# Graph layer on one core: a gather ring of eight thirds instead of six, key/value work six thirds later, weights loaded where they are used

## What is computed

```python
xn = _layernorm(x, axis=-1)
x = x + _L0_gnn_ref(xn, edge_attr_256, src, dst, gnn_weights, gnn_h_bias, 6250) \
      + _L0_mix_ref(xn[None], w_qkv, ..., w1, b1, w2, b2)[0]
x = x + _L0_ffn_ref(_layernorm(x, axis=-1)[None], Wr, br, W1, b1, W2, b2, gamma, beta)[0]
...
# gnn: over 106,250 edges sorted by dst
m = src_feats[src_idx] @ weights[:d] + edge_feats @ weights[d:]
norm = where(deg > 0, rsqrt(max(deg, 1)), 0)
h = segment_sum(m * norm[dst_idx][:, None], dst_idx) + h_bias
# mix: linear attention with 8 heads, layer norm of k and v
kv = einsum('bhnd,bhne->bhde', ln(k), ln(v)) / HW
h = gelu((einsum('bhnd,bhde->bhne', q, kv) + x) @ w1 + b1) @ w2 + b2 + x
# ffn: one router for all rows picks 2 of 8 experts (256 -> 512 -> 256)
```

## Time and profile before

| | |
|---|---|
| three runs | 1624.92, 1627.36 (median), 1629.15 us |
| the profiled execution | 1632.06 us |
| its span | 1630.3 us |
| granted TensorE clock, mean share | 0.872 |
| busy in the span | PE 1173.3, PEld 803.1, POOL 915.7, DVE 654.6, ACT 559.7 us |
| moved | 295.03 MB, mean 181 GB/s |

### The profile page before, as it was taken

How to read it: one execution, slowest core, us unless ns; L and a number is a source line. 1 busy time by engine, 2 the same in 40 slices (tenths; PEclk the granted TensorE clock), 3 DMA queues, 4 the chain that set the end, 5 groups by cost and what they waited for, 6 DMA issues and landing times.

```text
span 1630.3 us, 22836 instructions
## 1 busy us (share of the span) xinstructions
PE 1173.3 (72%) x7416; PEld 803.1 (49%) x7416; DVE 654.6 (40%) x1698; ACT 559.7 (34%) x1157; POOL 915.7 (56%) x975
## 2 busy tenths in 40 slices
PE   0157767776686777766676767677776839999997
PEld 0033333433343343334445444453554539999997
DVE  5633223323223333221233244243432446676775
ACT  4731111111111111111333343333342457677674
POOL 6166666666666666666666666666666103344342
PEclk9988987888788888778798897889898959999999
DMA  9976666656665666486677787777777341222221
GB/s 234 319 216 202 181 194 185 205 177 180 201 193 174 189 199 181 127 260 204 206 225 232 220 240 248 225 223 241 234 225 238 103 136 40 71 61 76 64 68 39
DMA packets 209235, 295.03 MB, mean 181 GB/s; under 512 B 20940, under 2 KB 180146, under 8 KB 207887
## 3 DMA queue, kind: packets, MB, share of 16 engines
q1 hardware_dynamic: 152899, 165.66, 34.7%
q0 software_dynamic: 39888, 108.97, 22.1%
q10 hardware_dynamic: 16350, 19.20, 3.5%
HBM read 261.75 MB, written 32.00 MB: 180 GB/s over the span
## 4 chain that ended last, share of the span: by engine, by line
another core or an unknown queue 31%; PE 30%; issue 14%; DVE 9%; ACT 9%; DVEq 2%; DMA 2%; SPq 2%; ACTq 1%; POOL 0%; POOLq 0%
PE bank L1156 8%; PE bank L1167 8%; PE bank L944 2%; PE bank L997 2%; PE bank L938 2%; DVEq L1324 2%; PE bank L930 2%; PE bank L1003 1%; ACT fl L649 1%; PE bank L1041 1%; ACT L751 1%; ACT L731 1%; DVE acc L1326 1%; DVE xc L1339 1%
## 5 line engine op out<-in xcount | busy, mean ns | idle before, releaser
L583 POOL DMA_INDIRECT ring<-xn_table,src_sb x807 | 781.8, 969 | 465.7 <-issue 221.1
L930 PE MATMUL bank<-ring,s 128*32 128x512 f32 x1662 | 283.6, 667 | 65.3 <-DVE s L1298 42.6
L944 PE MATMUL bank<-fl_t,wg 128*128 128x128 f32 x1120 | 158.7, 300 | 51.6 <-ACT fl_t L649 36.7
L944 PEld LDWEIGHTS bank<-fl_t,wg 128*128 128x128 f32 x1120 | 146.7, 211 | 54.8 <-ACT fl_t L649 38.8
L938 PE MATMUL bank<-ident,fl 128*128 128x128 f32 x280 | 60.9, 356 | 146.9 <-ACT fl L649 131.7
L1326 DVE TENSOR_TENSOR acc<-acc,bank 128x96 f32 x277 | 70.7, 255 | 226.5 <-issue 87.4
L938 PEld LDWEIGHTS bank<-ident,fl 128*128 128x128 f32 x280 | 39.3, 177 | 222.2 <-ACT fl L649 170.7
L1331 DVE TENSOR_TENSOR xt_lo<-bank,xt_hi 128x250 fp32r<-128x250 f32 (+1 forms) x75 | 37.9, 505 | 260.7 <-ACT xt_hi L649 173.0
L649 ACT ACTIVATE xt_hi<-bank 128x250 fp32r<-128x250 f32 (+1 forms) x75 | 33.4, 446 | 285.6 <-remote 227.3
L712 ACT ACTIVATE kvn<-xc 125x512 f32<-125x512 f32 x50 | 31.5, 630 | 262.1 <-DVE xc L1339 135.3
L1156 PE MATMUL bank<-xf_hi,fw_hi 128*128 128x256 f32 x400 | 113.5, 284 | 9.4 <-DVE fw_lo L1628 7.2
(11 more groups left out here) (221 smaller groups left out, 2374.1 us busy)
## 6 DMA issues: line engine op xcount, KB each, us to landing
ring<-edges SPq DMA_DIRECT2D x207, 512.0 KB
ring<-xn_table,src_sb POOLq DMA_INDIRECT x807
xnr<-xn_table SPq DMA_DIRECT2D x50, 125.0 KB
xnr<-xn_table SPq DMA_DIRECT2D x25, 250.0 KB
xch<-x SPq DMA_DIRECT2D x25, 250.0 KB
base_rows<-xch ACTq DMA_DIRECT2D x25, 250.0 KB
x_rows<-xch ACTq DMA_DIRECT2D x25, 250.0 KB
xt_cols<-xte ACTq DMA_DIRECT2D x25, 250.0 KB
```

The costliest lines, as they stand in the source:

```text
L583: pool.indirect_dma_start(out=to, out_offset=None, in_=rows, in_offset=bass.IndirectOffsetOnAxis(ap=index, axis=0),).then_inc(done, 16)
L930: mm = pe.matmul(ps_seg[t % 2][j * W:(j + 1) * W, :], lhsT=s32[:, t % 3, j * TS + i, :].bitcast(F32), rhs=ring[:, u, j, :], start=i == 0, ...
L944: mm = pe.matmul(ps_y[:, o * P:(o + 1) * P], lhsT=wg[:, c, o * P:(o + 1) * P], rhs=fl_t[:, c, :], start=c == 0, stop=c == 3)
```

## The change

The ring gets two more slots, and 32 KB per partition are found for them by laying buffers over each other. `RAW`, which was `RS`, stays at six. KV0 goes from 2 to 8; through it FOLD becomes 112, MIX runs from 120 to 207, and FIN from 42 to 71 (the number of steps stays 225). SP issues the weights at the steps at which they are next needed, and DVE and ACT prepare the kv weights at step 7, inside the loop.

```diff
-RS = 6
+RS = 8
...
-RAW = RS
+RAW = 6
...
-KV0 = 2
+KV0 = 8
...
-        xch = sbe("xch", [TN, XC, 2, D])
...
+        chunk_rows = sbm("chunk_rows", [P, XC, 2, D])
...
+        xch = chunk_rows[0:TN, :, :, :]
+        fold_flat = chunk_rows[:, :, :, :].rearrange("p c j d -> p (c j d)")
+        wq_sb, w1_sb, p_sb = (fold_flat[:, k * KC * D:(k + 1) * KC * D].rearrange("p (c d) -> p c d", d=D) for k in range(3))
...
@@ SP, mix_load @@
                 if c < XN:
                     sp.wait_ge(s_xt, NT)
+                    sp.wait_ge(s_c, 6)
...
@@ SP @@
             for q in range(RAW):
+                if q == 3:
+                    sp.wait_ge(s_rel, 1)
+                    sp.dma_start(wg[:, :, :], wgnn.rearrange("(c p) d -> p c d", p=P)).then_inc(s_wg, 16)
                 edge_load(q)
-            sp.wait_ge(s_rel, 1)
...
             sp.wait_ge(s_tab, TABLE_DONE)
...
             for q in range(TS * STEPS):
                 if RAW <= q < NQ:
                     edge_load(q)
+                if q == RAW:
+                    key_weights()
+                if q == RAW + 2:
+                    mix_weights()
...
@@ ACT @@
             for h in range(2):
...
-                act.wait_ge(s_gve, h + 1)
-                nc.scalar.activation(sdg[:, tiles], veg[:, tiles], ACT.Sqrt).then_inc(s_gsd, 1)
-                act.wait_ge(s_gr, h + 1)
+                act.wait_ge(s_vx0, NB + h + 1)
+                nc.scalar.activation(sdg[:, tiles], veg[:, tiles], ACT.Sqrt).then_inc(s_sx0, 1)
+            for h in range(2):
+                tiles = slice(h * RAW * ST // 2, (h + 1) * RAW * ST // 2)
+                act.wait_ge(s_r1, NB + h + 1)
...
-            act.wait_ge(s_wprep, 2)
-            copy(wkv_hi[:, :, :], wstage[:, :, :]).then_inc(s_wsplit, 1)
...
+                if q == KV0 - 1:
+                    act.wait_ge(s_wprep, 2)
+                    copy(wkv_hi[:, :, :], wstage[:, :, :]).then_inc(s_wsplit, 1)
...
@@ PE @@
                     if t == 1:
-                        pe.wait_ge(s_par, 16 * 11)
+                        pe.wait_ge(s_wg, 16)
...
@@ DVE @@
-            raw_stats(0)
-            raw_stats(1)
-            raw_scales(0)
-            raw_scales(1)
...
+            one_hot(0)
+            raw_stats(0)
+            raw_stats(1)
+            raw_scales(0)
+            raw_scales(1)
...
+                    if t == 1:
+                        v.wait_ge(s_zero, 1 + NB)
                     sums(t - 1)
+                if q == KV0 - 1:
+                    key_weights()
+                if q == KV0 + 6:
+                    row_bias()
```

More of the change, by code:

```diff
@@ L234, in gps_layer @@
         DEG = 3 * P
+        xch = chunk_rows[0:TN, :, :, :]
+        fold_flat = chunk_rows[:, :, :, :].rearrange("p c j d -> p (c j d)")
+        wq_sb, w1_sb, p_sb = (fold_flat[:, k * KC * D:(k + 1) * KC * D].rearrange("p (c d) -> p c d", d=D) for k in range(3))
+        kv_t = fold_flat[:, 3 * KC * D:3 * KC * D + KC * P].rearrange("p (c n) -> p c n", n=P)
+        floor = fl[0:1, 0:NS]
+        st6 = fl[0:TN, 288:288 + 6 * BLK].rearrange("p (j s) -> p j s", s=6)
+        mvs = fl[0:TN, 352:352 + 4 * BLK].rearrange("p (h j s) -> p h j s", h=2, s=2)
+        RT = RAW * ST
+        raw_flat = fl_t[:, :, :].rearrange("p c n -> p (c n)")
+        st6g = raw_flat[:, 0:6 * RT].rearrange("p (k s) -> p k s", s=6)
+        mvg = raw_flat[:, 6 * RT:8 * RT].rearrange("p (k s) -> p k s", s=2)
+        veg, sdg, rg, nmrg = (raw_flat[:, k * RT:(k + 1) * RT] for k in range(8, 12))
         sum_row = kvn[0:1, :, :].rearrange("p a (b d) -> p (a b) d", d=D)
@@ L258, in gps_layer @@
             "st", "mv", "vx0", "sx0", "rc0", "r1", "xn", "xnp", "tab", "zero"))
-        s_gst, s_gmv, s_gve, s_gsd, s_grc, s_gr, s_raw = (sem(f"s_{n}") for n in ("gst", "gmv", "gve", "gsd", "grc", "gr", "raw"))
-        s_id, s_const, s_iota, s_mask, s_d, s_dp, s_rel, s_wprep, s_wsplit = (sem(f"s_{n}") for n in (
-            "id", "const", "iota", "mask", "d", "dp", "rel", "wprep", "wsplit"))
+        s_raw = sem("s_raw")
+        s_id, s_const, s_iota, s_mask, s_d, s_dp, s_rel, s_wprep, s_wsplit, s_wg = (sem(f"s_{n}") for n in (
+            "id", "const", "iota", "mask", "d", "dp", "rel", "wprep", "wsplit", "wg"))
         s_e, s_gat = ([sem(f"s_{n}{u}") for u in range(RS)] for n in ("e", "gat"))
@@ L464, in _, with key_weights @@
-            sp.dma_start(hrows[:, :], hbias.partition_broadcast(TN)).then_inc(s_par, 16)
-            sp.dma_start(wr_sb[:, :, :], wr.rearrange("(c p) e -> p c e", p=P)).then_inc(s_rw, 16)
-            sp.dma_start(rt[0:1, 0, :], br.partition_broadcast(1)).then_inc(s_rw, 16)
-            sp.wait_ge(s_tab, TABLE_DONE)
+            sp.wait_ge(s_tab, TABLE_DONE)
+            def key_weights():
+                sp.dma_start(wstage[:, :, :], wkv_l.rearrange("(c p) d -> p c d", p=P)).then_inc(s_wkv, 16)
+                sp.dma_start(bkv[:, :], bkv_l.partition_broadcast(TN)).then_inc(s_wkv, 16)
+                for j, row in enumerate((kln_g, vln_g, kln_b, vln_b)):
+                    sp.dma_start(lns[:, j, :], row.partition_broadcast(P)).then_inc(s_par, 16)
@@ L958, in fold_weights @@
                 if step == 0:
+                    pe.wait_ge(s_par, 16 * 10)
                     pe.wait_ge(s_cs, 4)
```

86 lines of the change are left out of this document (38 added, 48 removed).

## The result

| | before | after |
|---|---|---|
| median of the runs | 1626.14 us (4 runs) | 1635.13 us (4 runs, 1634.52 to 1638.71) |
| ratio, 95% interval | | 1.0052 [1.0032, 1.0072] |
| profiled execution, span | 1632.06, 1630.3 us | 1638.71, 1636.9 us |
| third 8 summed | 117.2 us | 112.7 us |
| third 206 summed | 1289.5 us | 1284.3 us |

What follows compares the result with a forecast made beforehand. It took the bound to be a cycle: PE's completions arrive late while POOL streams gathers, with the ring full of landed data. Terms −14 +5 +0 −3 +2 +2 = −8 gave 1619.4 us on the median; 8-in-10 range 1600 to 1635.

Steps and rivals of the forecast that it cites:

- mix six steps later: Last thirds and tail: MIX ends at 207, not 201, so two more chunks fall there; +2 us, bounds 0 and +5.
- the start: Before the loop and its first steps: without early kv work third 8 is summed at about 103.6; −14 us, bounds −17 and −8.5.
- filling the slots: Early loop: POOL issues 8 more gathers before first pausing, while PE's completions are late; +5 us, bounds 0 and +10.
- the prediction's own sign of being wrong: Early loop: third 8 summed later than 110 us, where near 104 would show the forecast right.
- fold gate: SP at step 120: `mix_load(0)` waits for step 118, edge loads queue behind, at most one delay; +2 us, bounds 0 and +6.
- third rival: Early loop: filling the ring takes 10 us and eats the start's gain; −3 us in all, 1624.4, no change; chance 0.14.
- Steady state: Main loop: two more landed thirds give PE nothing, period stays 5.9 to 6.0 us per third; 0, bounds −5 and +5.
- The reading behind it: Main loop: PE's completions reach others late while POOL streams gathers; the cycle's cost per third does not contain the ring's depth.
- The first rival: Main loop: pauses are a lack of slots, period falls from 5.95 towards 5.1; total 1450, or 1565 for a third; chance 0.12.
- The rival that made the kernel slower through the gate: SP at step 120: first edge load lands after 12 us, PE stands; price 12 to 15, 1631.4 to 1634.4; chance 0.12.
- End of the gathers: Last thirds, run without gathers at 4.6 us instead of 5.95: two more such thirds; −3 us, bounds −4 and 0.

Runs made afterwards that it cites:

- lead of six: Changed kernel with POOL's gathers held to six thirds ahead of PE, SP's edge loads keeping eight slots: 1632.13 us, ratio 1.0029 against the kernel before.
- second set: Changed kernel run again beside the kernel before on a 5.9 us chip, unaltered: 1633.72 us against 1627.34, ratio 1.0033.
- paced kernels: Changed kernel with mix chunks 9/8 of a group apart instead of 6/5; with eight slots 1480.63 to 1484.84 us on 5.07 us chips, ratios 1.0046 to 1.0067.

## Why the prediction was wrong

**The failed step is "mix six steps later, +2, bounds 0 and +5".** The tail grew by 11.7 us, and by 13.1 in the second trace. I had put PE's work of a chunk at some 4 us and taken the tail for a place where a little of it lies bare. Two terms were too small. First, two more chunks in the last thirds can lay twice that work bare, 8 us, by the prediction's own figure, and the bound was +5; from third 206 to the last projection 7.9 us more were measured. Second, the closings were not in the sum at all: four chunks are turned behind the last projection, not two, one after the other, about 4 us each, and that gives 4.1 us more. What stands between two turns is a chain through PE, DVE and ACT. The table of group numbers in the source would have told the count ahead: with FIN starting at 42 the last four closings are at 68 to 71, so that four turns fall behind the last edges.

That the placing of the side work makes the loss is shown: KV0 = 2 takes it away (1.0003 against 1.0033 and 1.0052 on 5.9 us chips, 0.9987 and 0.9992 against 1.0061 on 5.07 us chips), and KV0 = 8 alone puts it on the kernel before (1.0103), with the tail of the changed one.

**The second step that failed is the start, −14, with +5 for filling the slots.** Third 8 came at 112.7 and 110.1, so −4.5 and −7.1 of the −14, and the prediction's own sign of being wrong, third 8 later than 110, came true. That it came at 103.0 with a lead of six does not make the size right for six slots: there the same late signal only falls behind third 9, and by third 12 all three stand 6 to 7 us ahead of before. So the mechanism behind the +5 was right (PE's signals are late while POOL streams), but it is not the two more slots that bring it on. By third 206 the loop was to be 12 us ahead (−14, +5 and −3, not counting the fold gate); by the medians it is about 3 us ahead (estimated above), and by the same reckoning 7 us in the second set. Third 8 was also no fair milestone: by then the kernel before has done kv work that the changed one does later. My third rival (−3 in all, no change) described the loop up to there better than the forecast.

**Steady state, 0: right.** 5.92 against 5.91 us per third, 90 pauses. The reading behind it (completions are seen late while gathers stream) held against its rivals: the half-gather run, the signal at 108.27, and the updates of one kernel on two chips say the same. The first rival, pauses for lack of slots, falls on this chip. The Trainium skill, Perfetto Trace Analysis, section on optimization strategy, has the repeated gap as a possible sign of too few buffers; here the gaps stayed at eight slots (123.8 and 73.3 us), so here it was not that.

**Fold gate, +2 with bounds 0 and +6: held.** SP was held for 26 us (35 forecast), and PE waited once, 4.95 us at third 121, without falling behind; in two more traces there was no such wait. The rival that made the kernel slower through the gate did not occur. The sign of the result came from a place for which I had no rival.

**End of the gathers, −3:** not separable from the start in the traces; the changed kernel sums thirds 201 to 206 at 4.1 us each (1263.7 to 1284.3), the one before at 4.6.

## What to carry to other kernels

Where side work rides on a loop by fixed steps, moving its first step moves its last one, and what falls behind the loop's end has no cover: count the dependent closings behind the last shared step, engine by engine, before pricing the start. A buffer ring that is full of landed data gains nothing from depth, and a head start that nobody on the critical path waits for is not passed on. One early milestone can mislead about such a head start; look at a few later ones too. Packing the side work closer to save the tail can give the saving back inside the loop.

## What the runs showed of the hardware

The kernel before took 1474 to 1476 us on some chips and 1625 to 1627 on others (medians), with gathers of the same length. On the slower ones PE's semaphore updates came late while POOL issued gathers back to back: those behind the projections at a median of 4.1 to 5.5 us after the last matmul's recorded end (six traces with all gathers), against 0.01 us on the faster ones; those of ACT and DVE did not (none over 0.1 us). In one case ACT could take up a finished PE instruction only after 8.6 us (99.65 to 108.29). PE's waits for the group copies were 103.5 us there, on a faster chip 14.1 in the same kernel; leaving out half the gathers brought a slower chip to 1293 us and the median lateness to 0.03. What distinguishes the chips was not found, nor whether the issuing of gathers or their transfers do it.

The sign held on both classes: the changed kernel against the same with KV0 = 2 is 0.3 to 0.5% slower on the one (across sets) and 0.6 to 0.7% on the other. The two slots of the ring show no gain on a 5.9 us chip (1.0033 against 1.0029 with a lead of six). On 5.07 us chips the paced kernels with six slots or a lead of six have 1.0090 and 1.0093 against 1.0046 to 1.0067 with eight, so there the depth may be worth about 0.3%, though the unpaced pair (1.0067 with six slots, 1.0061 with eight) does not show it.
